# A state-space block on one core: which engine makes the inflow of a unit's first three state indices

## What is computed

```python
dbc = u @ Wdbc.T                        # splits into dlt (64), B (16), C (16) per token
delta = softplus(dlt @ Wdt.T + bdt)     # per token and feature
for n in range(16):                     # decay exp(delta*A[n]), inflow delta*u*B[n]
    h[n][t] = exp(delta[t]*A[n]) * h[n][t-1] + delta[t]*u[t]*B[n][t]
y = sum_n(h[n] * C[n]) + u * D
out = x + gate * ((silu(mx)*y1 + silu(mx)*y2) @ Wf.T + bf + skip)
```

## Time and profile before

| | |
|---|---|
| median of 3 runs | 3401.86 us (3401.29 to 3406.7) |
| the profiled execution | 3410.34 us |
| its span in the profile | 3408.4 us |
| VectorE busy | 3090.2 us, 91% |
| TensorE matmul busy | 2982.9 us, 88% |
| GpSimd busy | 2982.0 us, 87% |
| ScalarE busy | 2667.4 us, 78% |
| granted TensorE clock, mean | 0.965 of full speed |

### The profile page before, as it was taken

How to read it: one execution, slowest core, us unless ns; L and a number is a source line. 1 busy time by engine, 2 the same in 40 slices (tenths; PEclk the granted TensorE clock), 3 DMA queues, 4 the chain that set the end, 5 groups by cost and what they waited for, 6 DMA issues and landing times.

```text
span 3408.4 us, 49569 instructions
## 1 busy us (share of the span) xinstructions
PE 2982.9 (88%) x17232; PEld 2142.3 (63%) x17232; DVE 3090.2 (91%) x1983; ACT 2667.4 (78%) x5070; POOL 2982.0 (87%) x1352
## 2 busy tenths in 40 slices
PE   8987888898888888888888888898888888888898
PEld 3554666666666666666666666666666666666665
DVE  2546999999999999999999999999999999999995
ACT  0336898988788898987777898988777898987772
POOL 1335999999999999999999999999999999999996
PEclk9988999999999999999999999999999999999999
DMA  5575344744557344645457334645457344644463
GB/s 217 177 251 186 127 138 141 236 157 164 176 189 261 131 139 142 237 143 168 158 199 249 131 134 145 231 150 162 158 197 255 125 143 141 225 155 161 152 214 114
DMA packets 215920, 594.67 MB, mean 174 GB/s; under 512 B 21276, under 2 KB 67548, under 8 KB 211320
## 3 DMA queue, kind: packets, MB, share of 16 engines
q1 hardware_dynamic: 213224, 572.63, 49.7%
q0 software_dynamic: 2304, 16.78, 1.3%
q10 hardware_dynamic: 144, 2.10, 0.2%
HBM read 510.79 MB, written 80.63 MB: 174 GB/s over the span
## 4 chain that ended last, share of the span: by engine, by line
DVE 27%; PE 25%; POOL 21%; issue 17%; ACT 1%; DVEq 0%; POOLq 0%; ACTq 0%
POOL hbuf L1201 16%; DVE slot L1298 15%; DVE hbuf L1298 8%; PE y L868 7%; POOL bst L1196 5%; PE mb L950 4%; PE mb L839 3%; PE slot L879 3%; DVE hbuf L1303 2%; DVE delta L1240 2%; PE slot L890 2%; PE mb L849 1%; PE mb L941 1%; PE mb L909 1%; ACT abuf L1101 1%
## 5 line engine op out<-in xcount | busy, mean ns | idle before, releaser
L1201 POOL TENSOR_TENSOR hbuf<-hbuf,cres 128x1024 f32<-128x1024 f32 x640 | 1507.5, 2375 | 174.5 <-DVE hbuf L1298 173.7
L1196 POOL TENSOR_TENSOR bst<-bst,du 128x1024 f32<-128x1024 f32 x576 | 1359.3, 2376 | 62.5 <-DVE du L1250 60.9
L868 PE MATMUL y<-ident,hbuf 128*128 128x128 f32 x8192 | 1096.3, 282 | 86.7 <-POOL hbuf L1201 86.5
L868 PEld LDWEIGHTS y<-ident,hbuf 128*128 128x128 f32 x8192 | 968.5, 146 | 251.8 <-POOL hbuf L1201 165.3
L1298 DVE TENSOR_TENSOR_SCAN hbuf<-dec,slot 128x1024 f32<-128x1024 f32 x448 | 1019.5, 2276 | 80.9 <-PE slot L890 58.3
L1101 ACT ACTIVATE abuf<-dut,bt 128x128 f32<-128x128 f32 x3072 | 971.1, 387 | 0.0
L1298 DVE TENSOR_TENSOR_SCAN slot<-slot,bst 128x1024 f32<-128x1024 f32 x384 | 875.5, 2280 | 13.2 <-ACT slot L1160 12.6
L1160 ACT ACTIVATE slot<-delta,par 128x1024 f32<-128x1024 f32 x576 | 639.9, 1111 | 232.6 <-DVE hbuf L1303 212.7
L879 PE MATMUL slot<-ident,abuf 128*128 128x128 f32 x3072 | 426.1, 284 | 208.8 <-ACT abuf L1101 173.9
L1160 ACT ACTIVATE dec<-delta,par 128x1024 f32<-128x1024 f32 x448 | 510.9, 1140 | 96.0 <-DVE hbuf L1298 96.0
L879 PEld LDWEIGHTS slot<-ident,abuf 128*128 128x128 f32 x3072 | 356.4, 145 | 341.1 <-ACT abuf L1101 201.4
(11 more groups left out here) (152 smaller groups left out, 2207.1 us busy)
## 6 DMA issues: line engine op xcount, KB each, us to landing
bst<-bc_s SPq DMA_DIRECT2D x576, 512.0 KB, 3.8
cres<-bc_s SPq DMA_DIRECT2D x128, 512.0 KB, 7.0
wzs<-wz_s SPq DMA_DIRECT2D x64, 256.0 KB
yf_s<-yrd SPq DMA_DIRECT2D x32, 512.0 KB, 5.3
ybuf<-yf_s SPq DMA_DIRECT2D x32, 512.0 KB, 4.7
yg_s<-ybuf SPq DMA_DIRECT2D x31, 512.0 KB, 4.4
si_s<-silu SPq DMA_DIRECT2D x28, 512.0 KB, 6.0
silu<-si_s SPq DMA_DIRECT2D x28, 512.0 KB, 5.3
```

The lines of the kernel that those rows point to most:

```text
L868: last = nc.tensor.matmul(y[:, j * P:(j + 1) * P], hbuf[:, q % HR, j * P:(j + 1) * P], ident[:], start=False, stop=(q % N == N - 1), is_tr ...
L1196: nc.gpsimd.tensor_tensor(bst[:, i % BR, :], bst[:, i % BR, :], du[:, k % 2, :], ALU.mult).then_inc(pool_b, 1)
L1201: nc.gpsimd.tensor_tensor(hbuf[:, q % HR, :], hbuf[:, q % HR, :], cres[:, q % N, :], ALU.mult).then_inc(pool_prod, 1)
```

## The change

The kinds become `"EVEVAVAPAVAPAPAV"`. Chunks 0 and 2 are of kind E, chunk 1 is V, so a unit has five V chunks and two E chunks. `diag` holds two sets of 8 diagonal matrices, the second of which ScalarE makes at chunk 0 of the first unit of a group. The tile of `bst` that this takes in SBUF is given up: BR is 4. DR is 2, so an inflow is made two GpSimd chunks ahead. The copy of `dut` waits for the unit's last spread. From chunk 6 on, by the same rules as above, GpSimd's order is now: product 6, 7, inflow 11, product 8, inflow 13, products 10, 11, inflow 15, products 12, 13, inflow 1', product 14, inflow 3', product 0', inflow 5', product 2'.

```diff
--- before.py
+++ after.py
@@ -464,14 +464,14 @@
                 project(1, c, ps[c % 2])
 
 
-KINDS = "VEVVAVAPAVAPAPAV"
+KINDS = "EVEVAVAPAVAPAPAV"
 SCALE_STEPS = {0: (4, 0), 2: (4, 1), 3: (6, 0), 5: (6, 1), 6: (8, 0), 7: (8, 1),
                8: (10, 0), 9: (10, 1), 10: (12, 0), 11: (12, 1), 12: (14, 0), 13: (14, 1)}
-SPREAD = KINDS.index("E")
+SPREAD = [n for n in range(N) if KINDS[n] == "E"]
 SEQ = ET * N
 HR = 4
-DR = 3
-BR = 5
+DR = 2
+BR = 4
 KD = R + N + 1
 
 
@@ -518,7 +518,7 @@
             "soft", "ud", "yrd", "silu", "ybuf", "dec", "dut"))
         abuf = sb("abuf", [P, 2, S])
         bt = sb("bt", [P, 2, ET, N])
-        diag = sb("diag", [P, ET, P])
+        diag = sb("diag", [P, len(SPREAD), ET, P])
         wf = sb("wf", [P, ET, D])
         wx = sb("wx", [P, D])
         skip, xres, gateb = (sb(n, [P, D]) for n in ("skip", "xres", "gateb"))
@@ -544,7 +544,7 @@
         delta_ready, du_ready, scanned, dve_prod, silu_ready, gated, proj_read = (sem(n) for n in (
             "delta_ready", "du_ready", "scanned", "dve_prod", "silu_ready", "gated", "proj_read"))
         pool_b, pool_prod, res_step, out_ready = (sem(n) for n in ("pool_b", "pool_prod", "res_step", "out_ready"))
-        diag_ready = sem("diag_ready")
+        diag_ready = [sem(f"diag_ready{i}") for i in range(len(SPREAD))]
         xc_in, pj_in, dbc_mm, dbc_ready, dbc_out = (sem(n) for n in (
             "xc_in", "pj_in", "dbc_mm", "dbc_ready", "dbc_out"))
         block = ctx.enter_context(nc.Block())
@@ -883,11 +883,12 @@
             def spread_inflow(q):
 
                 pe.wait_ge(dut_ready, 2 * (q // N) + 2)
-                pe.wait_ge(diag_ready, q // SEQ + 1)
+                i = SPREAD.index(q % N)
+                pe.wait_ge(diag_ready[i], q // SEQ + 1)
                 if q >= 2:
                     wait_scanned_out(pe, q - 2)
                 for j in range(ET):
-                    last = nc.tensor.matmul(slot[q % 2][:, j * P:(j + 1) * P], dut[:, j * P:(j + 1) * P], diag[:, j, :],
+                    last = nc.tensor.matmul(slot[q % 2][:, j * P:(j + 1) * P], dut[:, j * P:(j + 1) * P], diag[:, i, j, :],
                                             start=True, stop=True)
                 last.then_inc(turned, 1)
 
@@ -1108,18 +1109,19 @@
                 nc.scalar.activation(bt[:, g % 2].rearrange("p e n -> p (e n)"), bank[:, 0:ET * N],
                                      ACT.Copy).then_inc(bt_ready, 1)
 
-            def make_diagonal(g):
+            def make_diagonal(g, i):
+                n = SPREAD[i]
                 act.wait_ge(bt_ready, g + 1)
                 if g > 0:
-                    act.wait_ge(turned, before("AE", (g * ET - 1) * N + SPREAD + 1))
+                    act.wait_ge(turned, before("AE", (g * ET - 1) * N + n + 1))
                 for j in range(ET):
-                    last = nc.scalar.activation(diag[:, j, :], ident[:], ACT.Copy, scale=bt[:, g % 2, j, SPREAD:SPREAD + 1])
-                last.then_inc(diag_ready, 1)
+                    last = nc.scalar.activation(diag[:, i, j, :], ident[:], ACT.Copy, scale=bt[:, g % 2, j, n:n + 1])
+                last.then_inc(diag_ready[i], 1)
 
             def copy_dut(k, h):
                 act.wait_ge(dut_mm, 2 * k + h + 1)
                 if k > 0:
-                    act.wait_ge(turned, before("AE", (k - 1) * N + SPREAD + 1))
+                    act.wait_ge(turned, before("AE", (k - 1) * N + SPREAD[-1] + 1))
                 if k > 0:
                     act.wait_ge(scaled, len(SCALE_STEPS) * k - 1 + h)
                 nc.scalar.activation(dut[:, half(h)], mb[h], ACT.Copy).then_inc(dut_ready, 1)
@@ -1138,7 +1140,8 @@
                 skip_half(0, h)
             for h in range(2):
                 copy_dut(0, h)
-            make_diagonal(0)
+            for i in range(len(SPREAD)):
+                make_diagonal(0, i)
 
             for k in range(NU):
                 f, zs = wtile(k), z_step(k)
@@ -1159,6 +1162,8 @@
                         decays = slot[q % 2][:]
                     nc.scalar.activation(decays, delta[:, k % 2, :], ACT.Exp,
                                          scale=par[:, f // ET, f % ET, PA + c:PA + c + 1]).then_inc(decay_ready, 1)
+                    if c == 0 and k > 0 and k % ET == 0:
+                        make_diagonal(k // ET, 1)
                     if c in SCALE_STEPS:
                         scale_half(N * k + SCALE_STEPS[c][0], SCALE_STEPS[c][1])
                     if c == 1 and k > 0 and has_mx(k - 1):
@@ -1177,7 +1182,7 @@
                         if c == zs + 4 and new_b:
                             copy_bt((k + 1) // ET)
                         if c == 14 and new_b:
-                            make_diagonal((k + 1) // ET)
+                            make_diagonal((k + 1) // ET, 0)
                         if c == zs + 5:
                             copy_dut(k + 1, 0)
                         if c == min(zs + 7, N - 1):

```

## The result

The changed kernel takes 3498.55 us (median of 4 runs, 3497.19 to 3509.49), against 3404.28 for the kernel before in the same session: ratio 1.0284, 95% interval 1.0261 to 1.0308. The forecast was slower, 3477 us with a range of 3405 to 3520; the loss is 94 us where 75 were forecast. The profiled execution took 3509.49 us, with a span of 3507.7; it is the longest of the four, 11 us above the median, and the lines and unit lengths of the changed kernel are read from it.

A forecast was written before the change was run, and what follows sets the result against it. VectorE was taken as nearly saturated, GpSimd close behind and tied to it once per unit. Forward +19, backward +48, boundaries +3 and start +5 gave +75 us on the 3401.86 median: 3477 us, range 3405 to 3520 (forecast's own 3450 to 3510).

The forecast's parts named there:

- What VectorE saves: VectorE's queue: one V chunk fewer in each of 64 units, 1.28 us each, 82 us in all.
- Product 12 is one instruction later: GpSimd's queue: inflow 15 moves behind product 11, so product 12 ends 2.33 us later, moving the backward block by that much.
- The spread at chunk 0': TensorE's queue, behind sum 12 and the first block: scan 0' waits 1.10 us in forward units, about 3.5 in backward.
- ScalarE's chain to the decays of 3': Unit head: later decays make scan 3' wait, 0.86 us more lost in forward units and 0.7 in backward.
- Forward units: 28 units, each 0.7 us longer (1.28 saved, 1.96 waited): +19 us.
- Backward units: 27 units at 1.63 us longer, plus 0.6 more in six of the first sequence: +48 us.
- a rival with 0.06: TensorE falls to 1.2 GHz behind product 12's wait: 5.2 us more in 27 backward units, about 3618 us; chance 0.06.
- Boundaries: Seven boundaries between groups, where ScalarE makes a second set of diagonals: +0.5 us each, +3 in all.
- the start with its low clock: Scan 0 of unit 0 waits for both diagonal sets, first boundary at low clock: +5 us together, bounds 0 and 8.
- the tail itself: End of unit 63: zero cost, since GpSimd waits there for VectorE.
- The price of the spread: TensorE: 1.78 us per spread from the trace, taken over 3.5 us estimated from the skill's fourfold fp32 transpose speed.

The follow-up runs named there:

- dr3_alone: The changed kernel with inflows made three ahead again (DR 3), four B tiles and both spreads kept: 3407.11 us, ratio to the kernel before 0.9999.
- before_dr2: The kernel before the change with only DR set from 3 to 2, kinds and five B tiles unchanged: 3513.16 us, ratio 1.0310.
- one_spread_at_0: The kernel before the change with its one spread at chunk 0 instead of chunk 1: 3406.52 us, ratio 1.0001.
- the zeros: Ten zero matmuls before sum 12 in units behind a backward one: added to the changed kernel 3481.27 us, to that with the late copy of y 3465.63.
- copy_y_late: The changed kernel with ScalarE's copy of y behind the decays of chunk 3 instead of in front: 3510.18 us, ratio 1.0306.
- one_spread_at_0_copy_y_late: The kernel before with its single spread at chunk 0 and the copy of y behind the decays of chunk 3: 3435.69 us, ratio 1.0085.
- dr3_copy_y_late: The changed kernel with DR 3 and the copy of y behind the decays of chunk 3: 3377.63 us, ratio to the kernel before 0.9915.

## Why the forecast came out as it did

The forecast for the median was 3477 us, and 3498.55 were measured, inside the forecast's own 3450 to 3510. The two profiled executions differ by 99 us where the sum had 75. By the unit lengths TensorE's clock took those 24 us; the other deviations, of 1 to 5 us each, cancel, and that is luck.

*What VectorE saves.* Right, and the kernel never got it: 82 us of VectorE's queue were removed, and its waits grew by more.

*Product 12 is one instruction later.* Right, and the main step. In backward units it was forecast to move the block by 2.33 us; two opposite tests, dr3_alone and before_dr2, show 2.3 us a backward unit each, with and without the new kinds.

*The spread at chunk 0'.* Right in place and size: waits of 1.04 and 3.40 us against 1.10 and 3.5 forecast, and in one_spread_at_0 the signs by kind of unit.

*ScalarE's chain to the decays of 3'.* Right: 0.78 and 0.60 us, against 0.86 and 0.7.

*Forward units* were summed to +19 us and measured +20.3 over 28 units.

*Backward units* are the mis-sized term: +48 forecast for 27, +69.1 measured over the 26 that lie between two `finish_delta`. The step that fell short is the price of the wait for product 12, taken at full clock. TensorE's fall to 1.2 GHz had stood beside it as a rival with 0.06, priced at 5.2 us in all 27 units. It came, in 15 of the 26, and at 1.6 us each: in the unit shown the granted clock was 1.00 again from 1762 on, and the projection's block, from 1760.94, took 4.00 us instead of 3.60. The rival had the place and the wait right, and its price and number of units too high. At 50.4 us, the forecast's own length, the sum is 20 x (50.4 - 48.8) + 6 x (50.4 - 48.2) = 45, and about 15 x 1.6 = 24 of clock give the 69. That the zeros take the 1.6 us away and leave the rest shows the split.

*Boundaries* cost +5.7 us instead of 3, all seven counted. The first two lengths behind the setup cost +1.8, where the start with its low clock had 5. That 3 + 5 and 5.7 + 1.8 nearly agree is luck. The setup was 2.1 us shorter in this execution, and 4.6 us come behind the last `finish_delta`, where the last backward head and the tail lie; I had put the tail itself at zero, and it was not tested apart. Together: 20.3 + 69.1 + 5.7 + 1.8 - 2.1 + 4.6 = 99.4, the difference of the two spans being 99.3.

*The price of the spread.* In the changed kernel a spread is followed by the next sum after 1.78 us (1712.71 to 1714.49 in the backward unit shown), so the price of the trace stood and not that of a factor of four.

What stays open is why the clock fell behind a wait of 2.3 us in one backward unit and not in the next. The lengths alternate nearly regularly in the changed kernel; in before_dr2, with the same waits of 2.3 us for product 12, 21 of the 26 backward units are without a fall behind it, in copy_y_late 3. Nothing was run to tell what decides it.

## What to carry to other kernels

When two engines are both near full, the order of the second one's queue matters as much as the number of its instructions: find the instruction on it that another engine's queue waits for, and count what stands between. Moving a make-ahead distance from three to two cost 3% here and gave nothing back; the same change of kinds with the old distance, and with one copy moved out of the way, was 0.85% faster than the kernel before. When a wait is removed, look at once for the next one in line: here scan 5' took what scan 4' gave back, and a later copy of y made TensorE stand and lose its clock.

## What the runs showed that I had not expected

A wait of 2.3 us on TensorE was followed by a granted clock of 0.50 in some units and by 1.00 in others. For the copied y, waits of 1.76 us were followed by a fall in 10 of 28 forward units (copy_y_late), those of one_spread_at_0_copy_y_late, mostly 1.94 us, in all 28, and those of 1.30 us in none of 28 (dr3_copy_y_late), while two boundaries of that run fell behind two waits in a row of 1.3 to 1.5 us. In the changed kernel a fall comes on top of the wait, at 1.6 us on the path for each. The 600 instructions that add zeros, 2.4 us of work a unit, took 17 us off the kernel. The Trainium skill says in TensorE: Matmul & The Clock Gate, Part 1, that activity is what releases the throttle, and the two runs with zeros agree with it.
